# Row maxima per score bank instead of per two banks, and another order of the steps, in a fused diffusion transformer block on one core

## The reference

```python
h = _ln(x) * (1 + sc_msa) + sh_msa
x = x + _self_attn(h, w_qkv, b_qkv, w_so, b_so) * g_msa
h = _ln(x) * (1 + sc_mca) + sh_mca
x = x + _topk_cross_attn(h, context, w_q, b_q, w_kv, b_kv, w_co, b_co) * g_mca   # top_k(scores, 16), softmax, gather of v
h = _ln(x) * (1 + sc_mlp) + sh_mlp
x = x + _swiglu(h, w_m1, b_m1, w_m2, b_m2) * g_mlp
...
xq = _ada_ln(x, t_vec, Wss_q, bss_q); xkv = _ada_ln(ctx, t_vec, Wss_kv, bss_kv)
scores = einsum('bqhd,bkhd->bhqk', xq @ Wq + bq, k) / sqrt(16)
return x + (einsum('bhqk,bkhd->bqhd', softmax(scores), v).reshape(B, Lq, H) @ Wp + bp)
```

## Time and profile before

| | us |
|---|---|
| median of three runs | 647.51 (647.25 to 649.8) |
| the profiled execution, its own time | 646.2 |
| its span in the trace | 644.1 |

### The profile page before, as it was taken

The page is one execution under the profiler, slowest core; times in us unless marked ns, Lnnn a source line. Parts: engine busy times, 40 slices in busy tenths (PEclk is TensorE's granted clock), DMA queues, the critical chain, the costliest instruction groups (busy, mean ns, idle before and its releaser), DMA issues.

```text
span 644.1 us, 18326 instructions
## 1 busy us (share of the span) xinstructions
PE 611.9 (95%) x6029; PEld 526.9 (82%) x6029; DVE 539.8 (84%) x2281; ACT 495.0 (77%) x1907; POOL 366.1 (57%) x625
## 2 busy tenths in 40 slices
PE   6887999999999999999999999999999999989897
PEld 5676979788898989888898979888898978877785
DVE  2688898979899898989899998989899897969342
ACT  1765588788888888797888878788897888866265
POOL 3446564747567573855657484637647384646430
DMA  7870010120110101220102201010101100010000
GB/s 241 288 312 26 1 43 2 43 82 3 40 54 2 51 17 51 60 66 2 51 2 72 62 3 66 29 41 2 66 10 36 42 2 27 2 50 2 34 1 18
DMA packets 20540, 32.21 MB, mean 50 GB/s; under 512 B 2464, under 2 KB 11808, under 8 KB 20192
## 3 DMA queue, kind: packets, MB, share of 16 engines
q1 hardware_dynamic: 20448, 31.05, 14.9%
HBM read 28.85 MB, written 2.20 MB: 48 GB/s over the span
## 4 chain that ended last, share of the span: by engine, by line
PE 61%; DVE 19%; ACT 9%; POOL 5%; issue 3%; DMA 2%; SPq 1%; DVEq 0%; POOLq 0%; ACTq 0%
PE ring L1242 11%; PE ring L1081 10%; PE ring L1075 9%; PE ring L1199 8%; PE ring L1250 7%; PE s_bank L1186 6%; ACT probs L824 6%; PE ring L1219 5%; DVE left L989 3%; DVE left L1002 3%; DVE top L978 3%; PE ring L1133 2%; DVE top L996 2%; DVE neg_max L970 2%; POOL left L763 2%
## 5 line engine op out<-in xcount | busy, mean ns | idle before, releaser
L824 ACT ACTIVATE probs<-s_bank,neg_max 128x128 f32<-128x128 f32 x512 | 180.6, 404 | 8.3 <-DVE neg_max L970 7.3
L831 ACT ACTIVATE probs_t<-ring 128x512 f32<-128x512 f32 x192 | 112.5, 635 | 33.1 <-PE ring L1199 32.5
L824 ACT ACTIVATION_READ_ACCUMULATOR probs<-s_bank,neg_max 128x1 f32 x512 | 125.5, 245 | 0.0
L1242 PE MATMUL ring<-h_t,w_m 128*128 128x128 f32 x1024 | 123.3, 276 | 0.9 <-ACT probs_t L831 0.4
L1242 PEld LDWEIGHTS ring<-h_t,w_m 128*128 128x128 f32 x1024 | 118.2, 192 | 3.4 <-issue 2.5
L794 ACT ACTIVATE h_t<-ring,mod_all 128x128 f32<-128x128 f32 x160 | 64.9, 482 | 41.6 <-PE ring L1133 33.5
L821 ACT ACTIVATE probs<-s_bank,neg_max 128x128 f32<-128x128 f32 x256 | 75.4, 420 | 18.8 <-DVE left L989 18.8
L763 POOL TENSOR_TENSOR left<-left,probs 128x512 f32<-128x512 f32 x64 | 82.4, 1288 | 9.5
L970 DVE TENSOR_REDUCE neg_max<-s_bank 128x8 f32<-128x1024 f32 x64 | 76.9, 1210 | 9.1 <-PE s_bank L1186 8.9
L777 POOL TENSOR_TENSOR mlp<-mlp 128x512 f32<-128x512 f32 x32 | 40.7, 1272 | 66.8 <-ACT mlp L853 63.1
L1199 PE MATMUL ring<-ident,probs 128*128 128x128 f32 x512 | 70.6, 275 | 3.4 <-ACT mlp L853 0.7
(11 more groups left out here) (129 smaller groups left out, 1286.5 us busy)
## 6 DMA issues: line engine op xcount, KB each, us to landing
gates<-rows_dram SPq DMA_DIRECT2D x48, 256.0 KB, 3.7
x_res<-in_x SPq DMA_DIRECT2D x16, 128.0 KB, 3.7
ctx_in<-in_ctx SPq DMA_DIRECT2D x16, 128.0 KB, 3.3
ctx_t<-in_ctx_t SPq DMA_DIRECT2D x16, 128.0 KB, 3.1
w_m<-in_w_m SPq DMA_DIRECT2D x1, 2048.0 KB, 13.1
out_y<-x_res SPq DMA_DIRECT2D x16, 128.0 KB, 1.7
mlp<-in_w_ada SPq DMA_DIRECT2D x2, 512.0 KB, 6.7
w_m<-in_w_m SPq DMA_DIRECT2D x1, 1024.0 KB, 8.9
```

Of the source, the lines that this page charges most:

```text
L824: e = nc.scalar.activation(probs[:, k, u, j], s_bank[:, u, P * j:P * j + P], ACT.Exp, bias=neg_max[:, k, n:n + 1], accum_out=row_sum[:, k, ...
L831: nc.scalar.activation(dst, bank("T", which, b)[:], ACT.Relu if k == CROSS else ACT.Copy).then_inc(pt_ready, 1)
L1242: e = nc.tensor.matmul(d[:, P * j:P * j + P], w_m1[:, c, at:at + P], h_t[:, MLP, c], start=(c == 0), stop=(c == CK - 1))
```

## The change

Row maxima are taken per bank: `max` has four steps of 512 columns, and `exp` of a bank waits for its own. All five tables of order are new. The order of the attentions on `s_bank` is the same, and so are all other instructions; the fillers are still 20. Six of them stand in the head, one stands near the self scores of b14, 8 stand between the cross scores of b15 and the last `out`, and five behind it.

```diff
@@ the code
-                        act.wait_ge(maxed, DVE_N["max", (k, u // 2), b])
+                        act.wait_ge(maxed, DVE_N["max", (k, u), b])
...
                 if name == "max":
-                    k, half = which
-                    if half == 0:
+                    k, u = which
+                    if u == 0:
                         dve.wait_ge(scores_done, PE_N["scores", k, b])
-                    nc.vector.tensor_reduce(neg_max[:, k, 8 * half:8 * half + 8],
-                                            s_bank[:, 2 * half:2 * half + 2].rearrange("p u (j t) -> p (u j) t", t=P),
+                    nc.vector.tensor_reduce(neg_max[:, k, 4 * u:4 * u + 4], s_bank[:, u].rearrange("p (j t) -> p j t", t=P),
                                             AX.X, ALU.max, negate=True).then_inc(maxed, 1)
@@ one line of the tables, the others likewise
-    ("load", "ada0g", (70,)), ("load", "cond", (117,)), ("load", "so", (164,)), ("load", "vecs", (211,)),
+    ("load", "so", (70,)), ("load", "cond", (117,)), ("load", "ada0g", (164,)), ("load", "vecs", (211,)),
```

More of the change, by code:

```diff
@@ L58 @@
[L58 to L65, removed]
+    ("load", "qk", (446,)), ("load", "co", (493,)), ("load", "ctx0", (540,)), ("load", "ada1g", (587,)),
@@ L316 @@
-    ("mod_turn", CTX, (1063,)),
[4 rows of a table removed]
-    ("rows", CROSS, (1406,)),
-    ("turn", CTX, (1581, 4659, 5871, 12751, 16348, 19853, 23576, 27282,
-     30761, 34355, 37952, 41524, 45503, 49124, 52620, 56010)),
-    ("scores", SELF, (1606, 2548, 5303, 8593, 12118, 15667, 19372, 22941,
-     26513, 30126, 33734, 37210, 40889, 44461, 48082, 51690)),
-    ("keys", LAST, (1741, 5443, 6320, 13402, 16909, 20653, 24323, 27853,
-     31322, 35009, 38513, 42175, 45809, 49430, 52933, 56312)),
-    ("rows", MLP, (1831,)),
@@ new lines @@
+    ("rows", CROSS, (1426,)),
+    ("turn", CTX, (1601, 4134, 5883, 13123, 16280, 19785, 23485, 27191,
+     30675, 34266, 37870, 41442, 42731, 47089, 53483, 56775)),
+    ("scores", SELF, (1626, 2613, 5324, 8605, 12117, 15526, 19309, 22850,
[3 rows of a table added]
+    ("rows", MLP, (1850,)),
+    ("keys", LAST, (1940, 5202, 6332, 13373, 16841, 20585, 24046, 27762,
+     31326, 34827, 38431, 42371, 43272, 48313, 54029, 60722)),
+    ("keys", CROSS, (2030, 5112, 6242, 9760, 13283, 17118, 20675, 24136,
+     27672, 31236, 34917, 38521, 42003, 45263, 49497, 52565)),
@@ new lines @@
+    ("mods", CROSS, (3030,)), ("mods", MLP, (3085,)), ("mod_turn", CROSS, (3336,)),
+    ("turn", CROSS, (3399, 6217, 9600, 13098, 16816, 20298, 23996, 27512,
+     31186, 34777, 38406, 41953, 45444, 49109, 52423, 55829)),
+    ("q", CROSS, (3544, 6447, 9850, 13827, 17208, 20494, 24226, 28034,
+     31780, 35371, 38793, 42098, 46028, 49406, 52785, 56001)),
+    ("mod_turn", MLP, (3635,)), ("mods", LAST, (3647,)),
+    ("scores", CROSS, (3712, 6931, 10464, 14008, 17571, 21174, 24771, 28347,
+     31961, 35598, 39156, 42756, 46370, 49595, 53328, 56280)),
@@ new lines @@
+    ("mod_turn", LAST, (5908,)),
+    ("out", CROSS, (5947, 9239, 12737, 16319, 19849, 23524, 27103, 30714,
+     34305, 37909, 41481, 45175, 49136, 52199, 56092, 58515)),
+    ("turn", MLP, (6422, 9735, 13258, 16791, 20323, 24021, 27647, 31211,
[9 rows of a table added]
+    ("down", MLP, (8191, 11389, 15047, 18704, 22381, 25796, 29470, 33019,
+     36717, 40213, 44005, 47338, 51399, 54172, 58610, 60177)),
+    ("last", 0, (8980,)),
+    ("turn", LAST, (9176, 12673, 16255, 19810, 23460, 27078, 30650, 34241,
+     37845, 41417, 45105, 48200, 52135, 54917, 59488, 60903)),
```

650 lines of the change are left out of this document (326 added, 324 removed), and 34 rows, old and new, of tables (ACT_PLAN, DVE_PLAN, PE_PLAN).

## The result

The changed kernel takes 651.83 us in the median of nine runs (649.78 to 654.25), before in the same comparison 647.51 (nine runs, 645.26 to 649.8): a ratio of 1.0067 with an interval of 1.005 to 1.0085. It is slower by 4.3 us, where 5.8 us less were forecast. The profiled execution took 651.58 us, with a span of 649.4.

The account below looks back on a forecast made before the run. TensorE's own queue was taken to bound the middle, waits on others the tail. Terms -5.8 - 0.6 - 0.55 - 0.5 + 1.6 = -5.85 us against 646.2 gave 640.3, or 641.7 us by the median; range 637 to 648.

Parts of the forecast that it names:

- the six steps: Tail, TensorE's queue: six steps now stand behind the cross scores of b15 instead of ahead; -5.8 us.
- Rival (c): Cross scores of b15 waited for b13's exponentials, not TensorE's queue, so the 5.8 are lost; 646.2 or 647.5 us; chance 0.17.
- -0.6 and -0.55 on the chain behind the cross scores: b15's tail: b14's second MLP product moves behind the top-16 (-0.6); last exponentials wait for one bank's maxima (-0.55).
- The maxima: 64 reductions become 128 smaller ones: 5.1 us more on VectorE, 0 on the path; shorter ScalarE waits give -0.5 us.
- +1.6 for the trailing fillers: End of TensorE's queue: five fillers behind the last `out` instead of one end later than the store; +1.6 us.
- The head, 0 with 1.5 to either side: Head: loads, `mods CTX`, `v` and the zeroing of v change places; taken as 0, 1.5 us either way.
- The clock: Sign of being wrong: the granted clock leaves 1.00, since fewer fillers stand in the tail.
- Rival (d): VectorE becomes the bound through up to 9.6 us more work on the path of every sequence; 651.3 us; chance 0.09.

Follow-up runs that it names:

- second buffer: Changed kernel, order untouched, `x_norm` given a sixth part so the self-attention norm waits for the turn two sequences back; 643.26 us, ratio 0.9934.
- the two runs: Changed kernel with only `norm SELF b7` set back to its old number (644.49 us), and changed kernel with a second buffer for `x_norm` (643.26 us).
- two-bank maxima in the new order: Changed kernel with both norms moved back and four trailing fillers dropped, then two reductions of 1024 columns instead of four of 512; 643.88 us, ratio 0.9944.
- before with the fault put in: Kernel before with `norm SELF b7` moved ahead of the MLP products of b2 on GpSimd, `spread SELF b4` moved along; 653.48 us, ratio 1.011.
- norm b7 later: Changed kernel with one number of GpSimd's table, that of `norm SELF b7`, set to that of before; 644.49 us, ratio 0.9966.
- fillers in the stall: Changed kernel with four of its five trailing fillers moved between `turn SELF b6` and `down MLP b2`; 649.09 us, ratio 1.0027.
- no trailing fillers: Changed kernel with one filler behind the last `out` instead of five; 649.87 us, ratio 1.0033.
- the head's wait: Changed kernel with `norm SELF b7` put back and `norm CTX b2` moved behind `turn CTX b1` and the zeroing; 639.79 us, ratio 0.9902.

## Why the prediction was wrong

The direction was wrong, and it failed at a step that was left out, not at one that was mis-sized. The prediction says "So the middle is bound by TensorE's own queue and can hardly get shorter without less work", and under "The order, behind the middle" it compares the two orders from the scores of b13 on. That the middle can hardly get shorter was right. That it can get *longer* by a new order was asked only of VectorE. All five tables were new, and GpSimd's was not checked against TensorE's between 60 and 532 us. The sum has no term for it: the middle stands at nothing but for the reductions, and no reason is given for the other queues. There the early norm costs 8.5 us in the traces (the second buffer shows it) and 6.5 to 8.6 by the times of the two runs, more than all gains of the tail.

Point by point:

- **-5.8 from the six steps**: the starts show -5.9 from CROSS b12 to CROSS b15, nearly as summed. By the plans the work of TensorE ahead of CROSS b12 is the same in both to within 0.3 us, so this is the stretch to take. Rival (c) is refuted: the wait for the exponentials at that point is 0.73 us. But the order alone gives a little less: with two-bank maxima in the new order the stretch is 101.83 us, 4.8 under the 106.58 of before, and with four 100.75. So about 1.1 of the 5.9 belong to the maxima.
- **-0.6 and -0.55 on the chain behind the cross scores**: 60.41 instead of 61.14 us, a gain of 0.7 where 1.15 were summed. The link of the reduction came as forecast: from the last scores to the last `out` it is 11.44 us instead of 11.95, and 11.94 again with two-bank maxima in the new order. The product of b14 fell short: from the cross scores of b15 to its last scores it is 48.97 instead of 49.19 us, 0.2 of the 0.6; that link wasn't tried alone.
- **The maxima**: the reduction takes 0.674 us in the mean, in the range of 0.66 to 0.70. VectorE's busy sum rises by 5.6 us (5 to 10 forecast), and no run shows any of it on the path. The gain of 0.5 was too small: 1.6 us in the old order and 4 to 5 in the new one. The Trainium skill, page "VectorE: DVE Perf Modes", section on the TRN2 errata, gives (120 + 512) / 0.96 GHz = 0.658 us for this form; the trace agrees within 3%. Its warning that many small tiles pay the fixed part each (it names the latency of SBUF there, and this source is PSUM) is borne out for VectorE's busy time (2 x 0.674 is 0.13 us over one of 1.215), but the time got shorter; ScalarE waits 0.68 instead of 1.21 us at the place shown above.
- **+1.6 for the trailing fillers**: 1.9 in the trace, 2.0 by the run without them.
- **The head, 0 with 1.5 to either side**: the norm of the context ahead of the zeroing costs 2.1 us up to the end between two traces, 3.5 against their first scores and 4.7 by the medians, outside of it. Here too a norm of GpSimd waits for a turn; the prediction lists the zeroing as moved and doesn't ask what now stands ahead of it.
- **The clock**: "if the granted clock leaves 1.00, since fewer fillers stand in the tail". It left 1.00, but in the middle and the head, during the waits. In the tail it stays at 1.00 with the 8 fillers.
- **Rival (d)** gave 651.3 us, and 651.83 were measured. The number is a coincidence: its mechanism was VectorE's 64 more instructions, and those alone make the kernel faster.

With the two norms put back the same order takes 639.79 us, where the prediction had 641.7: 6.3 us under before in the same comparison, where 5.8 were forecast. That is partly luck, since the maxima gave 1 to 4 us more than their 0.5 and the moved steps and the chain some 1.5 less than their share.

## What to carry to other kernels

When a change replaces the order of several in-order queues, don't compare only the place where it seems to happen. For every step that waits for a buffer to be read (here each `norm` for the `turn` of the sequence before), look at what stands behind it in its own queue and at what the engine it waits for needs before it gets there. If the releasing step stands right ahead of one that needs something queued behind the wait, both engines stand still, even where GpSimd is only 56% busy. Where nothing urgent stands behind the wait it costs little: in before GpSimd waited 7.02 us and TensorE 1.25. Regular programs help: in the middle the norms of one kind come about every 3,500 numbers, and one that follows its predecessor by 460 is suspect at sight.

Where such a wait can't be placed safely, a second buffer takes it away without touching the order. Fillers behind the last output are part of the measured time.

## What the runs showed of the hardware

I hadn't expected the granted clock to fall inside the kernel. It did where TensorE stood for 4.1 to 5.9 us: in the kernel after (a wait of 5.93 us until 163.35, 0.50 from 161.3 to 168.0) and in before with the fault put in (4.92 us until 162.28, 0.50 from 160.2 to 166.6). The eight matmuls of `down` then take 6.02 and 5.95 us instead of 3.62. With fillers in the same gap, whose longest idle time is 1.54 us, the clock stays at 1.00. The Trainium skill, page "TensorE: Matmul & The Clock Gate", part on the clock gate, says that the array has a 1.2 GHz state that it takes when idle and a 2.4 GHz state when busy; the trace agrees with the levels. The cost was 2.4 us at the place (6.02 - 3.62); how much of it lasts to the end is not shown, at most 2 us by the run with the fillers.

The same wait doesn't always cost the same. The one of 4.11 us in the head stands in five of the kernels, and the two fillers behind it take 3.67 (after), 3.39 (norm b7 later), 2.59 (fillers in the stall), 3.63 (no trailing fillers) and 3.67 us (second buffer), where they take 1.97 at a clock of 1.00. And a stop that long isn't needed: near 13 us, where no wait of TensorE is over 1.9 us, the granted clock falls in seven of the twelve traces and not in the others; in the two rows shown with the head's wait it makes the step take 3.54 instead of 2.02 us and the first scores start 1.3 us later. So a difference of 1 or 2 us between two single traces is not to be put down to an edit without a look at the clock in the head.
